# Reordering the last two batches of a cross-attention kernel: U of batch 14 in halves around tile 10, and the last tile column half by column half

## The reference

```python
q = einsum('bte,ef->btf', x, Wq) + bq
k = einsum('bml,le->bme', ctx, Wk) + bk
v = einsum('bml,le->bme', ctx, Wv) + bv
w = softmax(einsum('bte,bme->btm', q, k) / sqrt(512), axis=1)   # over the 100 tokens
h = einsum('btm,bme->bte', w, v) + x
out = (h - mean(h)) * rsqrt(var(h) + 1e-6) * gamma + beta       # over the 512 columns
```

## Time and profile before

| | |
|---|---|
| three runs | 144.78, 145.21, 145.1 us, median 145.1 |
| profiled execution | 144.95 us, its span 143.2 us, mean granted TensorE clock 0.992 |
| TensorE matmul (PE) | 134.4 us busy, 94% of the span |
| VectorE (DVE) | 117.3 us, 82% |
| ScalarE (ACT) | 81.6 us, 57% |
| GpSimd (POOL) | 65.2 us, 46% |

### The profile page before, as it was taken

One profiled execution on the slowest core, in us unless ns is written; L12 is line 12 of the kernel. 1 busy time (PEld: TensorE's weight loads), 2 busy tenths in 40 slices (PEclk: granted clock), 3 DMA queues, 4 the chain that ended last, 5 costly groups with the idle time before them and its releaser, 6 DMA issues.

```text
span 143.2 us, 2969 instructions
## 1 busy us (share of the span) xinstructions
PE 134.4 (94%) x1046; PEld 129.4 (90%) x1046; DVE 117.3 (82%) x216; ACT 81.6 (57%) x286; POOL 65.2 (46%) x61
## 2 busy tenths in 40 slices
PE   6998999999899999999999999999999999999910
PEld 6998999999898999999999999999999999998900
DVE  0689989999777899759999975899699976876992
ACT  4677349459527836385564729475665628483520
POOL 1000000009031594735758472666667463659891
PEclk9999999999999999999999999999999999999996
DMA  4999999965057597897896889699897886545113
GB/s 141 300 406 421 421 300 395 317 213 194 5 205 237 195 307 243 328 346 259 314 311 259 322 256 402 215 316 326 252 306 250 331 273 225 217 146 178 73 73 146
DMA packets 10670, 37.33 MB, mean 261 GB/s; under 512 B 1184, under 2 KB 1184, under 8 KB 10656
## 3 DMA queue, kind: packets, MB, share of 16 engines
q1 hardware_dynamic: 9424, 34.92, 69.5%
q10 hardware_dynamic: 1232, 2.23, 4.1%
HBM read 33.87 MB, written 3.28 MB: 259 GB/s over the span
## 4 chain that ended last, share of the span: by engine, by line
PE 75%; DVE 10%; DMA 4%; POOL 3%; issue 2%; ACT 2%; SPq 1%; POOLq 1%
PE ps_U L400 28%; PE ps_S L386 27%; PE ps_Y L421 12%; DMA xT_in<-xT 4%; DVE xT_lo L647 3%; PE ps_U L361 3%; DVE xu L659 2%; PE ps_Y L361 2%; POOL xT_in L848 2%; PE ps_w L409 1%; SPq L255 1%; DVE wkq L637 1%; DVE W_lo L744 1%; POOL xT_in L836 1%; POOL rstd L841 1%
## 5 line engine op out<-in xcount | busy, mean ns | idle before, releaser
L521 ACT ACTIVATE expo<-scores,negmax 121x100 f32<-121x100 f32 x96 | 35.0, 366 | 27.3 <-DVE negmax L679 27.3
L386 PE MATMUL ps_S<-G,ctxT_in 128*121 128x100 f32 (+1 forms) x384 | 43.5, 270 | 0.0
L400 PEld LDWEIGHTS ps_U<-prob,ctx_in 121*128 121x128 f32 x360 | 42.1, 192 | 0.9
L400 PE MATMUL ps_U<-prob,ctx_in 121*128 121x100 f32 x360 | 42.5, 274 | 0.0
L386 PEld LDWEIGHTS ps_S<-G,ctxT_in 128*121 128x121 f32 (+1 forms) x384 | 42.0, 185 | 0.0
L825 POOL TENSOR_TENSOR prob<-expo,rinv 121x600 f32<-121x600 f32 x16 | 19.0, 1189 | 35.7 <-DVE rinv L686 35.7
L841 POOL TENSOR_TENSOR rstd<-vareps,neg_half 128x1 f32<-128x1 f32 (+1 forms) x13 | 12.4, 955 | 22.8 <-DVE vareps L717 22.5
L836 POOL TENSOR_TENSOR xT_in<-x_in,xT_in 128x512 f32<-128x512 f32 (+1 forms) x13 | 16.6, 1276 | 13.0 <-issue 8.4
L690 DVE TENSOR_REDUCE probsum<-prob 121x100 f32<-121x600 f32 x16 | 19.8, 1239 | 3.0 <-POOL prob L825 2.7
L521 ACT ACTIVATION_READ_ACCUMULATOR expo<-scores,negmax 121x1 f32 x96 | 18.0, 187 | 0.0
L675 DVE TENSOR_TENSOR scores<-ps_S,c_rows 121x600 f32<-121x600 f32 x16 | 12.5, 782 | 5.8 <-PE ps_S L386 5.6
(11 more groups left out here) (91 smaller groups left out, 175.8 us busy)
## 6 DMA issues: line engine op xcount, KB each, us to landing
ctx_in<-ctx SPq DMA_DIRECT2D x16, 768.0 KB, 5.7
ctxT_in<-ctxT SPq DMA_DIRECT2D x16, 722.0 KB, 5.2
xT_in<-xT SPq DMA_DIRECT2D x8, 400.0 KB, 8.8
x_in<-x SPq DMA_DIRECT2D x12, 256.0 KB, 4.7
out<-xT_in ACTq DMA_DIRECT2D x8, 256.0 KB, 4.2
wqk<-Wqk SPq DMA_DIRECT2D x4, 388.0 KB, 4.3
out<-xT_in SPq DMA_DIRECT2D x3, 256.0 KB, 2.0
wv_in<-Wv SPq DMA_DIRECT2D x1, 512.0 KB, 16.1
```

The costliest lines, as they stand in the source:

```text
L386: last = nc.tensor.matmul(ps_scores(c)[0:rows(c), :], ctxT_in[:, q, l * M + c * MP:l * M + c * MP + rows(c)], G[:, l, bass.ds(b * T, T)], ...
L400: last = nc.tensor.matmul(ps_U[:, q, l * T:(l + 1) * T], ctx_in[0:rows(c), q, c, l * P:(l + 1) * P], prob[0:rows(c), q, c * T:(c + 1) * T] ...
L521: last = nc.scalar.activation(expo[0:MP, q, c * T:(c + 1) * T], scores[0:MP, q, c * T:(c + 1) * T], ACT.Exp, bias=negmax[0:MP, q, c:c + 1] ...
```

## The change

The kernel keeps its computation and its amount of work. In the drain it does this:

1. TensorE: U of batch 14 goes in two halves like that of batch 15, `late_U(0)` to `late_U(3)`, and the order becomes `late_U(0)`, `weight_sum(11)`, `values(10)`, `late_U(1)`, `weight_sum(12)`, Y of tile 11 by l, `late_U(2)`, `late_U(3)`, Y of tile 12.
2. ScalarE and VectorE evict these four halves one by one (`late_upper`, `late_lower`), in new places of their lists; ScalarE has `scale_rows(10)` before the two halves of batch 15, where it was between them.
3. VectorE makes `lower_U(13)` and `normaliser(15)` before `centred_rows(9)`; GpSimd makes prob of 15 before `residual(10)`.
4. Tile 12 goes in two column halves of 256: 12 matmuls where there were 6, column half 0 in bank 0 of `ps_Y`, half 1 in bank 0 of `ps_S`. VectorE adds resid half by half and writes y back to `ps_Y`, so statistics and centring read it from PSUM. Centring of tile 11 is done by column halves as well.
5. VectorE scales tile 12 by halves; half 0 is stored from ScalarE's queue, half 1 from SP's.

The diff, cut to its core:

```diff
@@ -217,6 +221,13 @@
         def batch_tokens(b):
             return slice(b * T, (b + 1) * T)
+        LAST = NT - 1
+        EHALF = E // 2
+        halves = [slice(h * EHALF, (h + 1) * EHALF) for h in range(2)]
+        last_Y = [ps_Y[:, LAST % 2, 0:EHALF], ps_S[:, 0, 0:EHALF]]
+        last_y = [ps_Y[:, LAST % 2, halves[h]] for h in range(2)]
+        late_parts = [(b, l) for b in (B - 2, B - 1) for l in range(LC)]
         def rows(c):
             return ML if c == MC - 1 else MP
@@ -233,8 +244,8 @@
-        def each_turn(turn, first):
-            for b in range(first, B):
+        def each_turn(turn, first, last=B):
+            for b in range(first, last):
                 turn(b, b % 2)
         def exists(b):
@@ -306,12 +317,13 @@
                 if b < B:
                     next_ctx(b, b % 2)
-            for j in range(NT - 4, NT):
+            for j in range(NT - 4, NT - 1):
                 sp.wait_ge(result_set, j + 1)
-                source = scaled if j == NT - 1 else result
-                sp.dma_start(out_rows[tokens(j), :], source[0:tile_rows(j), j % 2, :]).then_inc(out_stored[j % 2], 16)
-            sp.wait_ge(out_stored[0], 16 * (NT - NT // 2))
+                sp.dma_start(out_rows[tokens(j), :], result[0:tile_rows(j), j % 2, :]).then_inc(out_stored[j % 2], 16)
+            sp.wait_ge(last_result_set, 2)
+            sp.dma_start(out_rows[tokens(LAST), halves[1]], scaled[:, LAST % 2, halves[1]]).then_inc(out_stored[LAST % 2], 16)
+            sp.wait_ge(out_stored[0], 16 * (NT - NT // 2 + 1))
             sp.wait_ge(out_stored[1], 16 * (NT // 2))
         @block.tensor
@@ -456,33 +468,60 @@
             pe.wait_ge(Wvlo_set, 1)
             each_turn(turn, 3)
-            weighted_ctx(B - 2, 0)
+            def late_U(n):
+                b, l = late_parts[n]
+                pe.wait_ge(ctx_loaded[b % 2], 8 * (b - b % 2) + 16)
+                pe.wait_ge(prob_set, b + 1)
+                if n < 2:
+                    pe.wait_ge(Ulo_set, B - 3 + l)
+                else:
+                    pe.wait_ge(late_Ulo_set, n - 1)
+                for c in range(MC):
+                    last = nc.tensor.matmul(ps_U[:, l, l * T:(l + 1) * T],
+                                            ctx_in[0:rows(c), b % 2, c, l * P:(l + 1) * P],
+                                            prob[0:rows(c), b % 2, c * T:(c + 1) * T], start=(c == 0), stop=(c == MC - 1))
+                last.then_inc(late_U_done, 1)
+            late_U(0)
             weight_sum(NT - 2)
             values(NT - 3)
-            values(NT - 2)
+            late_U(1)
             weight_sum(NT - 1)
-            pe.wait_ge(ctx_loaded[1], 8 * (B - 2) + 16)
-            pe.wait_ge(prob_set, B)
-            for l in range(LC):
-                pe.wait_ge(Ulo_set, B - 2 if l == 0 else B - 1)
-                for c in range(MC):
-                    last = nc.tensor.matmul(ps_U[:, 1 - l, l * T:(l + 1) * T],
-                                            ctx_in[0:rows(c), 1, c, l * P:(l + 1) * P],
-                                            prob[0:rows(c), 1, c * T:(c + 1) * T], start=(c == 0), stop=(c == MC - 1))
-                last.then_inc(last_U_done, 1)
-            pe.wait_ge(y_set, NT - 2)
+            pe.wait_ge(y_set, NT - 3)
             for l in range(LC):
                 for upart, vpart in ((U_hi, Wv_hi), (U_hi, Wv_lo), (U_lo, Wv_hi)):
                     if upart is U_lo:
-                        pe.wait_ge(last_Ulo_set, l + 1)
+                        pe.wait_ge(late_Ulo_set, l + 1)
                     else:
-                        pe.wait_ge(last_Uhi_set, l + 1)
-                    last = nc.tensor.matmul(ps_Y[:, (NT - 1) % 2, :], upart[:, l, tokens(NT - 1)], vpart[:, l, :],
+                        pe.wait_ge(late_Uhi_set, l + 1)
+                    last = nc.tensor.matmul(ps_Y[:, 1 - LAST % 2, :], upart[:, l, tokens(LAST - 1)], vpart[:, l, :],
                                             start=(l == 0 and upart is U_hi and vpart is Wv_hi),
                                             stop=(l == LC - 1 and upart is U_lo))
             last.then_inc(Y_done, 1)
+            late_U(2)
+            late_U(3)
+            pe.wait_ge(y_set, NT - 2)
+            pe.wait_ge(S_read, B)
+            def last_values(l, h):
+                for upart, vpart in ((U_hi, Wv_hi), (U_hi, Wv_lo), (U_lo, Wv_hi)):
+                    if upart is U_lo:
+                        pe.wait_ge(late_Ulo_set, l + 3)
+                    else:
+                        pe.wait_ge(late_Uhi_set, l + 3)
+                    done = nc.tensor.matmul(last_Y[h], upart[:, l, tokens(LAST)], vpart[:, l, halves[h]],
+                                            start=(l == 0 and upart is U_hi and vpart is Wv_hi),
+                                            stop=(l == LC - 1 and upart is U_lo))
+                return done
+            last_values(0, 0)
+            last_values(0, 1)
+            last_values(1, 0).then_inc(last_Y_done, 1)
+            last_values(1, 1).then_inc(last_Y_done, 1)
         @block.scalar
         def _(act):
@@ -603,17 +642,24 @@
             value_bias(0)
             exponentials(3, 1)
             each_turn(turn, 4)
+            def late_upper(n):
+                b, l = late_parts[n]
+                act.wait_ge(late_U_done, n + 1)
+                nc.scalar.activation(U_hi[:, l, batch_tokens(b)], ps_U[:, l, l * T:(l + 1) * T], ACT.Copy).then_inc(late_Uhi_set, 1)
             upper_U(B - 3, 1)
             value_bias(NT - 3)
+            late_upper(0)
+            value_bias(NT - 2)
             scale_rows(NT - 4)
-            upper_U(B - 2, 0)
-            value_bias(NT - 2)
+            late_upper(1)
             value_bias(NT - 1)
-            for l in range(LC):
-                act.wait_ge(last_U_done, l + 1)
-                nc.scalar.activation(U_hi[:, l, batch_tokens(B - 1)], ps_U[:, 1 - l, l * T:(l + 1) * T],
-                                     ACT.Copy).then_inc(last_Uhi_set, 1)
-                scale_rows(NT - 3 + l)
+            scale_rows(NT - 3)
+            late_upper(2)
+            late_upper(3)
+            scale_rows(NT - 2)
+            act.wait_ge(last_result_set, 1)
+            act.dma_start(out_rows[tokens(LAST), halves[0]], scaled[:, LAST % 2, halves[0]]).then_inc(out_stored[LAST % 2], 16)
         @block.vector
         def _(dve):
@@ -780,34 +826,70 @@
             row_stats(0)
             chunk_sum(2, 0)
             centre(0)
-            each_turn(turn, 4)
+            each_turn(turn, 4, B - 1)
+            lower_U(B - 4, 0)
+            normaliser(B - 2, 0)
+            maxima(B - 1, 1)
+            add_residual(NT - 4)
+            row_stats(NT - 4)
+            chunk_sum(B - 2, 0)
+            aggregate(NT - 4)
+            lower_U(B - 3, 1)
             normaliser(B - 1, 1)
-            lower_U(B - 3, 1)
-            lower_U(B - 2, 0)
+            centred_rows(NT - 4)
+            def late_lower(n):
+                b, l = late_parts[n]
+                dve.wait_ge(late_Uhi_set, n + 1)
+                nc.vector.tensor_tensor(U_lo[:, l, batch_tokens(b)], ps_U[:, l, l * T:(l + 1) * T],
+                                        U_hi[:, l, batch_tokens(b)].bitcast(F32), ALU.subtract).then_inc(late_Ulo_set, 1)
+            def centred_half(j, h, done):
+                q = j % 2
+                nc.vector.scalar_tensor_tensor(centred[:, q, halves[h]], y[:, q, halves[h]], meanvar[:, q, 0:1],
+                                               gamma_rows[:, halves[h]], ALU.subtract, ALU.mult).then_inc(done, 1)
+            def scale_and_shift(j, h, done):
+                q = j % 2
+                nc.vector.scalar_tensor_tensor(scaled[:, q, halves[h]], centred[:, q, halves[h]], rstd[:, q:q + 1],
+                                               beta_rows[:, halves[h]], ALU.mult, ALU.add).then_inc(done, 1)
+            late_lower(0)
             chunk_sum(B - 1, 1)
             add_residual(NT - 3)
+            late_lower(1)
             row_stats(NT - 3)
-            centre(NT - 3)
+            aggregate(NT - 3)
+            centred_rows(NT - 3)
             add_residual(NT - 2)
-            for l in range(LC):
-                dve.wait_ge(last_Uhi_set, l + 1)
-                nc.vector.tensor_tensor(U_lo[:, l, batch_tokens(B - 1)], ps_U[:, 1 - l, l * T:(l + 1) * T],
-                                        U_hi[:, l, batch_tokens(B - 1)].bitcast(F32),
-                                        ALU.subtract).then_inc(last_Ulo_set, 1)
-                if l == 0:
-                    row_stats(NT - 2)
-                    aggregate(NT - 2)
-            centred_rows(NT - 2)
-            add_residual(NT - 1)
-            row_stats(NT - 1)
-            centre(NT - 1)
-            q = (NT - 1) % 2
+            row_stats(NT - 2)
+            late_lower(2)
+            aggregate(NT - 2)
+            centred_half(NT - 2, 0, half_centred_set)
+            late_lower(3)
+            centred_half(NT - 2, 1, centred_set)
```

(29 more changed lines are left out.)

3 lines of the change are left out of this document (removed).

## The result

Over seven runs each the changed kernel takes 144.04 us in the median (143.55 to 144.57), the kernel before 145.21 (144.78 to 145.71). The ratio is 0.9931, with a 95% interval of 0.991 to 0.9952: faster by 1.0 us, 0.7 to 1.3. The profiled execution has a span of 142.3 us instead of 143.2.

A forecast was written before the change was run, and what follows sets the result against it. GpSimd, not TensorE, was taken to end the kernel. Terms -0.26 (GpSimd's end), +0.13 (scaling) and -0.33 (store) sum to -0.46 us, forecasting 144.5 us; own range 144.2 to 144.7, full range 144.0 to 145.4.

The forecast's parts named there:

- rival A: Prob of 15 starts before centring of tile 9, so GpSimd ends about 0.6 us earlier; time 144.0 us, chance 0.12.
- GpSimd's end: Last tile: GpSimd free at 139.1, centring not held, rstd(12) at 139.70 against 139.96, so -0.26 us.
- Scaling in halves: VectorE's scaling of tile 12: two halves end after 0.88 us instead of 0.75, so +0.13 for the second issue.
- Store in halves: Last store of tile 12: the last half moves for 0.34 us of the whole's 0.67, so -0.33.
- the low bound: Last store: of the bounds -0.33 and +0.3 us, the lower was taken because the stores' rate is near the loads'.
- TensorE's order: TensorE in the drain: the new order is a permutation whose waits are met, last tile at about 135.04 as before.
- the stall at the ninth matmul: Last tile on TensorE: the ninth matmul needs late_lower(3), adding 0.2 us; last matmul at 136.66 instead of 136.28.
- The slack of 0.2 us that I gave `chunk_sum(15)`: VectorE in the drain: chunk_sum(15) done by 130.6, in time for weight_sum(12) on TensorE at 130.77.
- B: Collisions and late U_hi keep rstd(12) at 139.96, or 1 KB rows cost like 2 KB; 144.7 to 145.1, chance 0.31.
- C: Half 0's store on ScalarE's queue lands late, 3.5 us instead of 2.0; +0.94 us, time 145.9, chance 0.05.
- D: Drain stalls because U_hi of batch 15 stands behind scale_rows(10) on ScalarE; 145.7 if 1.25 us late, chance 0.08.

The follow-up runs named there:

- e1: Kernel before with one edit: y of the last tile stays in PSUM; ratio to before 0.9947, drain 16.04 us against 16.50.
- e2: Changed kernel with y of the last tile in SBUF again; ratio to the kernel before 0.9963, drain 16.18 us against the changed kernel's 15.72.
- e5_order_only: Changed kernel with only the drain's order kept: last tile as six matmuls, y in SBUF, one scaling, one store; ratio to before 0.9987, drain 16.34 us.
- e3_one_store: Changed kernel with one scaling of 512 columns and one store of 256 KB; ratio to the kernel before 0.9958, drain 15.89 us.
- e4_prob_late: Changed kernel with prob of 15 behind residual(10) again and centring of tile 9 ahead of lower_U(13); ratio to before 1.0005, drain 16.65 us.
- e7_psum_all: Changed kernel with y of tiles 9 to 11 in PSUM too, TensorE waiting for their centring; ratio to before 0.993, drain 15.40 us.
- e8_scale_between: Changed kernel with scale_rows(10) between the two halves of U_hi of batch 15, as before the change; ratio to before 0.9942, drain 15.63 us.
- e9: Kernel before with e1's edit, plus last tile scaled and stored by halves from two queues; ratio to before 0.9953, drain 15.95 us.

## Why the prediction was right, and where its size was off

**Direction and mechanism** held. GpSimd ended the kernel, and most of what rstd(12) gained came from its last power op: 0.43 of 0.66 us, the other 0.23 from `finish(11)`, which ends 12.51 after `weight_sum(10)` instead of 12.74. vareps(12) ends 12.21 after `weight_sum(10)` against 12.26: as forecast, next to nothing. Centring from PSUM wasn't held, nor did it hold the power op; e1 and e2 show this from both sides at 0.46 us.

**The size** was off: -0.46 forecast, -0.78 in the trace (13.68 to 13.02 for rstd, then 0.18 more to the second issue and 0.3 less to landing), 144.5 against 144.04 us. The measured time lies below the forecast's own 144.2 to 144.7 and beside rival A's 144.0, though A's race went the other way; that it comes out at A's number is luck, since of the 1.0 us by which the runs moved 0.2 isn't in the drain. The term that failed is *GpSimd's end* with the power op behind it, -0.26, which measured -0.66. I had GpSimd free 0.08 us later than before (139.1 against 139.02), and it was free 0.23 earlier. What is in the difference, with 0.09 added to times of the changed kernel, which enters the drain that much earlier:

1. I let a held GpSimd operation begin its whole length after the port was free. It doesn't. Prob of 15 started at 127.51, centring ended at 127.35 + 0.74 = 128.09, and prob ended at 129.14, 1.05 later, where an unheld one takes 1.19. In e5_order_only the two `finish` ended 2.35 after the centring that held them, where the pair takes 2.58 before and 2.54 after the change. So 0.14 to 0.23 us of such an operation pass before the wait for the port begins, and each collision costs that much less. My own rows had this: a held power op ended 0.40 after the centring, an unheld one takes 0.55. I used the 0.40 for the power op and forgot it for prob. By the queue this moved the power op and the scaling of tile 10 and U_hi of half 2 (134.61 instead of the forecast 134.75).
2. vareps(11) came at 135.49, forecast 135.7: 0.14 of it is item 1, the rest is that `aggregate(11)` starts 0.08 before `late_lower(2)` ends, where I had put them one after the other.
3. I added 0.05 for half 1 of tile 11's centring, and rounded the two `finish` up. They ended 2.51 after the power op; `finish(10)` began at 136.16 and the half ended at 136.35, 0.19 later, so by item 1 `finish(10)` didn't feel it. And the record of the last power op begins 0.03 before that of `finish` ends, where I had put them one after the other.

Item 1 is read off the traces; I made no experiment that changes this lead time alone.

**Scaling in halves**: +0.13 forecast, 0.18 measured (1.00 from rstd to the second issue against 0.82). e3_one_store puts the cost of the split itself at 0.13; the other 0.05 is a later start of the scaling after rstd, 0.09 where it was 0.04, whose cause I leave open. **Store in halves**: -0.33 forecast, -0.3 measured. My reason for the low bound, a rate near the loads', is only partly true: 335 GB/s against 389. The line rate from 512 B on that the prediction quotes from the Trainium skill ("DMA: Bandwidth & Descriptors", "Specifications") isn't borne out between these two sizes of row. Its other figure, a fixed 2.0 us plus bytes / 436 GB/s, the Trainium skill ("DMA: Bandwidth & Descriptors", section "Anatomy of one DMA — SWDGE (gpsimd) path") gives for DMAs issued by GpSimd, not for these queues. As an estimate it makes 2.6 and 2.3 us of the two stores, where 2.0 and 1.7 were measured, and only the difference of 0.3 agrees.

**TensorE's order**: no stall before `late_U(1)` or `weight_sum(12)`, as forecast; the stall at the ninth matmul was 0.1, not 0.2, and the last one started at 136.57 by before's clock (136.48 + 0.09), forecast 136.66. The slack of 0.2 us that I gave `chunk_sum(15)` was 0.3 (130.42 to 130.72), and e4_prob_late shows what it costs when prob comes later than that.

**Rivals.** A (GpSimd wins the port) did not happen; the race went as I took it, with centring first. B (nothing left over) is not what happened, but it came close for the new order, which by itself gives 0.16 us. One reason stands in the traces: the centring of tile 9, which held a power op for 0.44 us before (0.99 against 0.55), now holds prob of 15 for as long (1.63 against 1.19), so that this collision has moved and not gone. How much of the order's worth it takes isn't shown, since e7_psum_all removes it together with the others. C did not happen: ScalarE's store landed in 1.7 us. The queue isn't what made the earlier store take 3.5: in e1, e2 and e3 that same store on ScalarE's queue landed in 2.0. That the loads around it did is likely and not tested. D exists as an order, and costs 0.08 us by e8_scale_between, not a stall. Three parts nearly make up the whole: 0.16 for the order (e5), 0.46 for the port (e1, e2) and 0.17 for the halves of scaling and store (e3) are 0.79, against 0.78. On top of e1 the halves gave only 0.09 (e9), so the sum isn't exact to better than 0.1.
